# Head variances of two attention passes: VectorE statistics in PSUM in place of ScalarE squares and VectorE sums

## The chip, the cores and the metric

The kernel runs on one NeuronCore of a Trainium2 chip. The metric is the device time of one execution in microseconds (us); lower is better. Five engines take part, each with its own queue of instructions that run in order: TensorE (PE in the profile, its weight loads PEld), VectorE (DVE), ScalarE (ACT), GpSimd (POOL) and SyncE (SP), which issues the DMAs. They wait for one another by semaphores alone.

## What is computed

A gated block over 16 sequences of 64 tokens with 256 features. A first cross attention and a feed-forward layer come ahead of what matters here. Then one attention layer runs twice over the 1024 tokens, as a pass over the block's own keys and values and as a cross pass over those of a context; an expert layer ends the kernel. The part that the change touches, cut from the reference:

```python
def _ln(x, w, b):
    mu = jnp.mean(x, axis=-1, keepdims=True)
    var = jnp.mean(jnp.square(x - mu), axis=-1, keepdims=True)
    return (x - mu) * jax.lax.rsqrt(var + EPS) * w + b
...
q = _fp8_linear_pertensor(ln_out, wq, wq_scale, q_in_scale).reshape(b, s, g, hpg, d)
q = _ln(q, qln_w, qln_b)
k = _fp8_linear_pertensor(ln_out, wk, wk_scale, k_in_scale).reshape(b, s, g, d)
k = _ln(k, kln_w, kln_b)
v = _fp8_linear_pertensor(ln_out, wv, wv_scale, v_in_scale).reshape(b, s, g, d)
core = _gqa(q, k, v).reshape(b, s, nh * d)
qx = _fp8_linear_pertensor(ln_out, wqx, wqx_scale, qx_in_scale).reshape(b, s, g, hpg, d)
qx = _ln(qx, qxln_w, qxln_b)
kvx = jnp.einsum('bsi,oi->bso', cond, w_kv_x)
```

There are 16 query heads and 8 key heads of d = 128 columns. Each head of each token is normalised by its own variance (`_ln`) before the scores.

## The kernel before

**Tiles.** A tile is 128 tokens (two sequences); each pass has 8 tiles, numbered 0 to 7 (own) and 8 to 15 (cross). A tile's projections come in chunks of 512 columns, four heads, each in one PSUM bank. In the own pass these are, by the index `i`: key 0, query 0, query 1, key 1, query 2, query 3 (the six that are normalised) and two chunks of values. In the cross pass only the four query chunks 1, 2, 4 and 5 are projected; keys and values are loaded from DRAM, where the start of the kernel has put them, and the keys' variances are made beforehand from a second load (`key_squares`, `key_sums`, `key_rstd`). The weights are centred per head when they are split, so that a head's mean is zero and its variance is the mean of its squares.

**The variance of a chunk, three engines long.** ACT squares the bank into SBUF (`square`, L1979), scaled so that the 128 squares of a head and one further column that holds epsilon add up to the variance plus epsilon. DVE adds the 129 columns of each of the four heads (`sums`, L1727). POOL raises the four results to the power -1/2 (`rstd`, L1615) into `g_rs`. Buffers for four such chunks are used in turn (`NORMS`).

**The scale, then the turn.** The chunk is multiplied by its heads' factors into `g_qn`: ACT does chunks 0 and 3 as four activations of 128 columns with a factor each (L2005), DVE does the query chunks 1, 2, 4 and 5 as one multiplication of 512 columns (L1740). PE transposes `g_qn` (`turn`, L2247), and ACT keeps the result, multiplied by the norm's weight and with its bias added (`keep_qk`, L2013, parameters `lnp`). `g_qn` has two buffers, so a scale waits for the turn of two chunks before. A PSUM bank is projected into again only after the scale of the chunk that it held.

**The rest of a tile.** Scores (L2258), the row maxima and their subtraction on DVE (L1746, L1750), the exponential on ACT (L2023), its sums on DVE (L1756), the division on POOL (`normalise`, L1625), a transpose of the probabilities (L2267), which ACT keeps (`keep_pT`, L2032), the product with the values (`attend`, L2284), then on DVE the rounding to fp8 in steps (`unload`, `clip`, `power`, `lift`, L1766 to L1782), finished on POOL (`g_cat`, L1636), and the output projection (L2303).

**The order is written out by hand** for each engine: `ahead(0)` starts tile 0, `both_own(n)` interleaves the attention of tile n with the projections of tile n + 1 = m, and `both_cross(n)` does so from n = 7 on. `ahead` also holds, among the work of tile 0, the context products (L2225), which ACT copies out (`keep_context`, L1986), and the rounding of token blocks on DVE (`round_tokens`, L1787 to L1795). In `both_own(1)`, `(3)` and `(5)` POOL centres a chunk of the cross pass's weights (`ctx.centre`, L185) between two `rstd` and `normalise`. Where several engines scale, `after_scale` makes a reader wait for the count of the engine that scaled the chunk: `kn_done` counts ACT's scales, `qn_done` DVE's. SP loads a tile's keys for the cross pass behind `kn_done`.

## Time and profile before

| | us |
|---|---|
| median of 3 runs | 634.34 (633.56 to 635.05) |
| span of the profiled execution, first to last instruction | 632.0 |
| PE busy in it | 576.7 |
| DVE busy | 494.6 |
| ACT busy | 369.1 |
| POOL busy | 365.9 |

The span is that of one profiled execution; what lies before the first and behind the last instruction of a run is not in it. A busy share is a mean over stages with different limits. Matmuls are pipelined, so PE that is busy is not PE at its peak, and the ends of matmuls are modelled. In the views below every line begins with a time in us from the start of the span, or with a line of the kernel; "out<-in" names what is written and read with sizes (partitions x elements), and "idle before <-releaser" is the time that the engine stood still ahead of the group and whose work ended it.

### The profile page before, as it was taken

The numbers are of one execution on the slowest core, as the hardware profiler recorded it, in microseconds if no ns is written. First come the engines' busy times: TensorE is split into PE (matmuls) and PEld (weight loads), VectorE is DVE, ScalarE is ACT, GpSimd is POOL, SyncE is SP. The second block draws the span as 40 slices with busy tenths as digits, with TensorE's granted clock in tenths as the row PEclk, the third lists the DMA queues.
The fourth block names the chain that finished last, engine by engine and source line by source line (L and its number), as shares of the span: only waits on it lengthen the run. The fifth ranks groups of instructions, "written<-read, shape, count | busy, mean of one in ns | idle before, by whom it ended". The sixth has DMA issues, their size and how long they took to land.

```text
span 632.0 us, 10614 instructions
## 1 busy us (share of the span) xinstructions
PE 576.7 (91%) x3735; PEld 468.2 (74%) x3738; DVE 494.6 (78%) x924; ACT 369.1 (58%) x669; POOL 365.9 (58%) x299
## 2 busy tenths in 40 slices
PE   3999679959869999999988999999999999999996
PEld 1664225635548888988977889888889888888886
DVE  4697999775999998999998889999997956333333
ACT  1559657757766776776766676667665235434221
POOL 4101495014578787868659967676777634855431
PEclk9999999988989999999998999999999999999999
DMA  7892113015512131031192141222210100310001
GB/s 219 272 348 77 60 50 117 34 67 152 180 33 106 35 111 58 1 134 35 48 357 96 37 124 57 86 84 85 59 43 18 35 0 3 117 37 30 1 2 67
DMA packets 44564, 54.87 MB, mean 87 GB/s; under 512 B 8416, under 2 KB 30816, under 8 KB 44512
## 3 DMA queue, kind: packets, MB, share of 16 engines
q1 hardware_dynamic: 44512, 54.20, 26.5%
q8 instruction: 30, 0.49, 0.3%
q14 instruction: 22, 0.18, 0.1%
HBM read 41.60 MB, written 12.58 MB: 86 GB/s over the span
## 4 chain that ended last, share of the span: by engine, by line
PE 64%; DVE 6%; POOL 3%; issue 3%; ACT 2%; DVEq 0%; POOLq 0%; ACTq 0%
PE g_proj L2217 13%; PE g_proj L2303 8%; PE g_scores L2258 7%; PE g_turn L2247 6%; PE g_op L2284 5%; PE g_op L474 3%; PE g_op L475 2%; PE g_op L476 2%; PE g_proj L459 2%; PE g_proj L461 2%; PE g_proj L460 2%; PE g_turn L2267 2%; PE g_op L2225 1%; POOL g_rs L1615 1%; PE g_turn L459 1%
## 5 line engine op out<-in xcount | busy, mean ns | idle before, releaser
L1615 POOL TENSOR_TENSOR g_rs<-g_ve,neg_half 128x4 f32<-128x4 f32 x80 | 83.7, 1052 | 36.4 <-DVE g_ve L1727 36.0
L1636 POOL TENSOR_TENSOR g_cat<-g_yb,g_kb 128x1024 fp32r<-128x1024 bf16 x32 | 70.9, 2224 | 41.3 <-DVE g_yb L1782 41.3
L2217 PE MATMUL g_proj<-w_hi,g_xqc 128*128 128x512 f32 x192 | 84.4, 439 | 6.7 <-ACT g_qn L2005 4.1
L2217 PE MATMUL g_proj<-w_lo,g_xqc 128*128 128x512 f32 x192 | 76.2, 397 | 0.0
L503 POOL TENSOR_TENSOR m_h_lo<-m_h,m_h_hi 128x512 fp32r<-128x512 f32 x32 | 41.4, 1297 | 57.1 <-ACT m_h_hi L490 57.1
L1727 DVE TENSOR_REDUCE g_ve<-g_sq 128x4 f32<-128x516 f32 x80 | 54.8, 685 | 16.9 <-ACT g_sq L1979 14.9
L2258 PEld LDWEIGHTS g_scores<-g_qkT 128*128 128x128 f32 x512 | 60.9, 192 | 2.7 <-issue 1.4
L2258 PE MATMUL g_scores<-g_qkT 128*128 128x64 f32 x512 | 61.0, 272 | 0.0
L2247 PE MATMUL g_turn<-ident,g_qn 128*128 128x128 f32 x384 | 58.2, 278 | 1.8 <-DVE g_qn L1740 1.5
L1979 ACT ACTIVATE g_sq<-g_proj 128x512 f32<-128x512 f32 x80 | 47.8, 597 | 16.7 <-PE g_proj L2217 15.2
L2247 PEld LDWEIGHTS g_turn<-ident,g_qn 128*128 128x128 f32 x384 | 44.8, 143 | 11.7 <-DVE g_qn L1740 3.6
L490 ACT ACTIVATE m_h_hi<-m_h 128x512 fp32r<-128x512 f32 x32 | 20.2, 632 | 48.6 <-DVE m_h L497 48.6
L2217 PEld LDWEIGHTS g_proj<-w_hi,g_xqc 128*128 128x128 f32 x192 | 36.8, 191 | 15.6 <-ACT g_qn L2005 5.0
L2013 ACT ACTIVATE g_qkT<-g_turn,c_lnp 128x512 f32<-128x512 f32 x48 | 36.6, 778 | 16.6 <-PE g_turn L2247 16.6
L1323 PE MATMUL f_bank<-f_w_ctx,f_ctxT 128*128 128x512 f32 x96 | 44.0, 594 | 0.9 <-ACT f_kept L1079 0.9
L1740 DVE TENSOR_TENSOR g_qn<-g_proj,g_rs 128x512 f32<-128x512 f32 x64 | 43.7, 682 | 1.3 <-POOL g_rs L1615 1.3
L2284 PE MATMUL g_op<-g_pT,g_v 64*128 64x128 f32 x512 | 37.2, 285 | 5.5 <-ACT g_pT L2032 5.5
L513 DVE SCALAR_TENSOR_TENSOR x_res<-g_op,m_we,x_res 128x256 f32<-128x256 f32 x64 | 27.8, 479 | 17.8 <-PE g_op L476 17.8
L2284 PEld LDWEIGHTS g_op<-g_pT,g_v 64*128 64x128 f32 x512 | 31.1, 187 | 14.4 <-ACT g_pT L2032 9.9
L555 POOL TENSOR_TENSOR ln_rstd<-ln_ve,neg_half 128x4 f32<-128x4 f32 x6 | 6.5, 1085 | 60.3 <-DVE ln_ve L542 60.3
L2217 PEld LDWEIGHTS g_proj<-w_lo,g_xqc 128*128 128x128 f32 x192 | 36.9, 192 | 5.6 <-issue 1.0
L2013 ACT ACTIVATE g_qkT<-g_turn,x_lnp 128x512 f32<-128x512 f32 x48 | 36.2, 771 | 5.6 <-PE g_turn L2247 5.6
(242 smaller groups left out, 1662.2 us busy)
## 6 DMA issues: line engine op xcount, KB each, us to landing
kvx_rows<-f_kept SPq DMA_DIRECT2D x24, 256.0 KB, 2.4
g_ksq<-kvx_rows SPq DMA_DIRECT2D x8, 512.0 KB, 4.5
g_kraw<-kvx_rows SPq DMA_DIRECT2D x16, 256.0 KB, 3.2
g_v<-kvx_rows SPq DMA_DIRECT2D x8, 512.0 KB, 4.2
m_raw<-in_L_W SPq DMA_DIRECT2D x16, 256.0 KB, 3.0
c_raw<-in_L_wqT SPq DMA_DIRECT2D x4, 512.0 KB, 6.2
f_w_ctx<-in_L_wkvxT SPq DMA_DIRECT2D x4, 512.0 KB, 8.0
c_praw<-in_L_wprojT SPq DMA_DIRECT2D x4, 512.0 KB, 5.6
```

Source lines behind the costliest of these rows:

```text
L1323: last = T.matmul(context_bank(e)[:], ctxT[:, c_, tile * P:(tile + 1) * P], w_ctx[:, chunk, c_, :], start=c_ == 0, stop=c_ == KT - 1)
L1615: G.tensor_tensor(rs[:, at % NORMS, :], ve[:, at % NORMS, :], k["half"][:, 0:4], ALU.pow).then_inc(q["rs_done"], 1)
L1636: G.tensor_tensor(cat[:, h].rearrange("p h (b s) -> p b h s", b=2), yb[:, h, :].rearrange("p (b h s) -> p b h s", b=2, s=SEQ), kb[:, h, :] ...
L1727: V.tensor_reduce(ve[:, at % NORMS, :], sq[:, at % 2], AX.X, ALU.add).then_inc(q["ve_done"], 1)
L1740: V.tensor_tensor(qn[:, i % 2, :].rearrange("p (h d) -> p h d", d=D), bank(n, i)[:].rearrange("p (h d) -> p h d", d=D), bcast(rs[:, at % N ...
L1979: A.activation(sq[:, at % 2, :, 0:D], bank(n, i)[:].rearrange("p (h d) -> p h d", d=D), ACT.Square, scale=D ** -0.5).then_inc(q["sq_done"], 1)
L2013: A.activation(qkT[:, n % 2, at:at + 4, :], turns[TURN_BANK[i]][:].rearrange("p (h m) -> p h m", h=4), ACT.Identity, bias=lnp[:, w + 1:w + ...
L2217: last = T.matmul(bank(n, i)[:], xqc[:, n % 2, view * KT + c_, :], w[:, c_, :], start=c_ == 0 and part == 0, stop=c_ == KT - 1 and part == 1)
L2247: last = T.transpose(out, qn[:, i % 2, h * D:(h + 1) * D], k["ident"][:])
L2258: last = T.matmul(sp_[:, (g * 2 + b) * SEQ:(g * 2 + b + 1) * SEQ], qkT[:, n % 2, 2 * kv + b, :], qkT[:, n % 2, HEADS + kv, rows], start=Tr ...
L2284: last = T.matmul(op[:, b, g * P:(g + 1) * P], v[rows, n % 2, kv * D:(kv + 1) * D], pT[rows, h, g, :], start=True, stop=True)
L2303: last = T.matmul(proj[OUT_BANK][:, 0:E], cat[:, h, hd % (2 * GH), :], w[hd // 4][:, hd % 4, :], start=hd == 0 and part == 0, stop=hd == H ...
```

## The change

- ACT's squares of both passes are gone, and with them their SBUF buffer; a filler of the same size keeps the addresses behind it.
- In their place DVE takes two statistics a chunk (`bn_stats`) straight from the PSUM bank, each over two heads of 128 columns, read in turn, column by column, so that its even elements are one head and its odd elements the other. One statistic gives, for its even and for its odd elements, a count, a mean and the sum of squared deviations.
- POOL takes the four sums of squared deviations (elements 2 and 5 of each six), adds 128 epsilon into `vp`, waits for that, and takes the power. This yields the factor without the square root of 128, by which the norm's weight (`lnp`) is multiplied once instead: two further small DVE operations on the own pass's weights, one on the cross pass's.
- ACT scales chunks 0, 2, 3 and 5 of each tile, DVE chunks 1 and 4. Counts and waits follow (`act_scales`, `after_scale`).

The diff, cut to its core:

```diff
+        for w in (0,) if self.cross else (0, 2):
+            V.tensor_scalar(self.lnp[:, w:w + 1], self.lnp[:, w:w + 1], D ** 0.5, None, ALU.mult).then_inc(self.scales, 1)
...
-        sq = sb("sq", [P, 2, 4, D + 1])
-        ve, rs, qn = sb("ve", [P, NORMS, 4]), sb("rs", [P, NORMS, 4]), sb("qn", [P, 2, CH])
+        sb("unused", [P, 984])
+        ve, vp = sb("ve", [P, NORMS, 2, 6]), sb("vp", [P, NORMS, 4])
+        rs, qn = sb("rs", [P, NORMS, 4]), sb("qn", [P, 2, CH])
...
+        def act_scales(n):
+            return (0, 2, 3, 5)
...
# rstd(n, i), POOL
-                    G.tensor_tensor(rs[:, at % NORMS, :], ve[:, at % NORMS, :], k["half"][:, 0:4], ALU.pow).then_inc(q["rs_done"], 1)
+                    G.tensor_scalar(vp[:, at % NORMS, :].rearrange("p (a b) -> p a b", b=2), ve[:, at % NORMS, :, 2::3], D * LN_EPS, None,
+                                    ALU.add).then_inc(q["vp_done"], 1)
+                    pool.wait_ge(q["vp_done"], at + 1)
+                    G.tensor_tensor(rs[:, at % NORMS, :], vp[:, at % NORMS, :], k["half"][:, 0:4], ALU.pow).then_inc(q["rs_done"], 1)
...
# sums(n, i), DVE
-                    dve.wait_ge(q["sq_done"], at + 1)
+                    dve.wait_ge(q["qkv_done"], projected(n, i))
                     if at >= NORMS:
                         dve.wait_ge(q["rs_done"], at - NORMS + 1)
-                    V.tensor_reduce(ve[:, at % NORMS, :], sq[:, at % 2], AX.X, ALU.add).then_inc(q["ve_done"], 1)
+                    for two in range(2):
+                        heads = bank(n, i)[:, two * 2 * D:(two + 1) * 2 * D].rearrange("p (h d) -> p d h", d=D)
+                        last = V.bn_stats(ve[:, at % NORMS, two, :], heads)
+                    last.then_inc(q["ve_done"], 1)
...
# ahead(n), DVE: scale(n, 2) and scale(n, 5) go; ACT:
-                    square(n, 0)
-                    square(n, 1)
                     scale(n, 0)
                     keep_context(1)
                     own_out.high(act, 2)
-                    square(n, 2)
                     keep_qk(n, 0)
                     keep_context(2)
                     over_scale(2)
-                    square(n, 3)
                     keep_qk(n, 1)
-                    square(n, 4)
                     keep_context(3)
+                    scale(n, 2)
                     scale(n, 3)
                     keep_qk(n, 2)
-                    square(n, 5)
...
                     for u in range(4, 8):
                         over_scale(u)
+                    scale(n, 5)
                     keep_qk(n, 4)
...
# both_own(n), DVE: scale(m, 2) and scale(m, 5) go; ACT, squares left out:
                     keep_qk(m, 0)
                     keep_pT(n, 0)
                     keep_qk(m, 1)
+                    scale(m, 2)
                     scale(m, 3)
                     keep_pT(n, 1)
                     keep_qk(m, 2)
                     keep_v(m, 0)
                     keep_qk(m, 3)
+                    scale(m, 5)
                     keep_qk(m, 4)
...
# both_cross(n), ACT: the same, scale(m, 2) ahead of scale(m, 3), scale(m, 5) last
```

## Rows read from the trace of the kernel before

**Rows 1.** The page: PE's busy time, share of the span, instructions.

```profile
PE 576.7 (91%) x3735; PEld 468.2 (74%) x3738; DVE 494.6 (78%) x924; ACT 369.1 (58%) x669; POOL 365.9 (58%) x299
```

**Rows 2.** Table by stretch: length, busy PE, PEld, DVE, ACT, POOL, clock, DMA.

```profile
247.50:268.20 20.70, 20.40 (x159) 17.83 (x158) 19.13 (x31) 14.53 (x28) 16.38 (x14) 1.00 0.09 26
268.20:289.60 21.40, 21.40 (x165) 18.80 (x164) 19.98 (x34) 14.96 (x29) 16.20 (x14) 1.00 0.29 99
...
410.77:429.48 18.71, 18.01 (x152) 16.32 (x151) 17.08 (x33) 12.16 (x26) 13.27 (x13) 1.00 0.24 71
```

**Rows 3.** Chain of waits, 264 to 311 us: start, length, work.

```profile
264.36 3.85 PE g_proj L2303 x32
...
281.49 1.86 PE g_proj L2217 x8
...
285.76 1.97 POOL g_rs L1615 x2
287.74 1.87 POOL x_raw L185
...
290.66 0.66 PE g_turn L2267 x4
```

**Rows 4.** Instructions in order of time, 154 to 186 us: start, length, engine, work.

```profile
154.18 0.60 PE L2247 MATMUL g_turn<-ident,g_qn 128*128 128x128 f32 x4
...
155.54 0.60 PE L2247 MATMUL g_turn<-ident,g_qn 128*128 128x128 f32 x4
...
157.60 0.59 ACT L1986 ACTIVATE g_late_kept<-g_op 128x512 f32<-128x512 f32 x1
...
174.37 0.69 DVE L1727 TENSOR_REDUCE g_ve<-g_sq 128x4 f32<-128x516 f32 x1 [1.22 <-ACT g_sq L1979]
...
175.80 0.69 DVE L1727 TENSOR_REDUCE g_ve<-g_sq 128x4 f32<-128x516 f32 x1 [0.74 <-ACT g_sq L1979]
...
185.25 0.50 PE L2217 MATMUL g_proj<-w_hi,g_xqc 128*128 128x512 f32 x1 [1.36 <-DVE g_qn L1740]
```

**Rows 5.** Groups by form, from 130 us: count, busy us, mean ns, idle before.

```profile
L1727 DVE TENSOR_REDUCE g_ve<-g_sq 128x4 f32<-128x516 f32 x80 | 54.8, 685 | 16.9 <-ACT g_sq L1979 14.9 <-issue 0.2
L1740 DVE TENSOR_TENSOR g_qn<-g_proj,g_rs 128x512 f32<-128x512 f32 x64 | 43.7, 682 | 1.3 <-POOL g_rs L1615 1.3
...
L328 DVE BATCH_NORM_STATS2 m_stats<-x_res 128x6 f32<-128x256 f32 x8 | 3.3, 413 | 0.0
...
L1979 ACT ACTIVATE g_sq<-g_proj 128x512 f32<-128x512 f32 x80 | 47.8, 597 | 16.7 <-PE g_proj L2217 15.2
...
L2005 ACT ACTIVATE g_qn<-g_proj,g_rs 128x128 f32<-128x128 f32 x64 | 18.3, 369 | 19.7 <-POOL g_rs L1615 19.7
```

**Rows 6.** Instructions in order of time on DVE, near 116 us.

```profile
116.34 1.41 DVE L536 BATCH_NORM_STATS2 ln_sums<-x_res 128x6 f32<-128x256 f32 x4
```

**Rows 7.** Groups by form on POOL, its smallest operations.

```profile
L310 POOL TENSOR_SCALAR_AFFINE_SELECT m_earlier<-m_earlier 128x49 f32<-128x49 f32 x1 | 0.3, 295 | 0.1
...
L1643 POOL MEMSET g_ksq<- 128x8 f32 x1 | 0.1, 108 | 0.0
```

**Rows 8.** Instructions in order of time on POOL, end of an own tile.

```profile
281.17 4.62 POOL L1636 TENSOR_TENSOR g_cat<-g_yb,g_kb 128x1024 fp32r<-128x1024 bf16 x2 [2.65 <-DVE g_yb L1782]
```

**Rows 9.** An own tile: POOL's second normalise, then PE in the chain of waits.

```profile
273.42 1.05 POOL L1625 TENSOR_TENSOR g_ex<-g_ex,g_rc 128x512 f32<-128x512 f32 x1
...
274.90 0.44 PE g_turn L2267 x4
```

**Rows 10.** Instructions in order of time, chunks 1 and 2 of an own tile.

```profile
271.48 0.77 ACT L2013 ACTIVATE g_qkT<-g_turn,c_lnp 128x512 f32<-128x512 f32 x1
...
273.33 0.66 PE L2247 MATMUL g_turn<-ident,g_qn 128*128 128x128 f32 x4
```

**Rows 11.** Instructions in order of time on ACT, a cross tile.

```profile
412.90 1.27 ACT L2005 ACTIVATE g_qn<-g_kraw,g_krs 128x128 f32<-128x128 f32 x4
...
415.27 0.60 ACT L2032 ACTIVATE g_pT<-g_turn 128x512 f32<-128x512 f32 x1 [0.28 <-PE g_turn L2267]
```

More of the change, by code:

```diff
@@ L192, in high @@
             act.wait_ge(self.loaded[n], 16)
-        act.wait_ge(self.scales, 4 if self.cross else 6)
+        act.wait_ge(self.scales, 5 if self.cross else 8)
         for c_ in range(KT):
@@ L1496, in after_scale @@
                 return
-            if i in (0, 3):
-                eng.wait_ge(q["kn_done"], n * 2 + i // 3 + 1)
-            else:
-                eng.wait_ge(q["qn_done"], n * NP + (1, 2, 4, 5).index(i) + 1)
+            act = i in act_scales(n)
+            done = sum((i_ in act_scales(n_)) == act for n_ in range(n + 1) for i_ in range(NN if n_ < n else i + 1))
+            eng.wait_ge(q["kn_done"] if act else q["qn_done"], done)
         def measured(n, i):
@@ L1639, in ahead @@
                 def ahead(n):
-                    G.memset(sq[:, :, :, D:D + 1], LN_EPS).then_inc(q["eps_made"], 1)
                     copy_tile(0)
@@ L1822, in ahead @@
                     early_tokens()
-                    dve.wait_ge(q["eps_made"], 1)
                     sums(n, 0)
@@ L1829, in ahead @@
                     sums(n, 2)
-                    scale(n, 2)
                     sums(n, 3)
@@ L1838, in ahead @@
                     late_tokens(1)
-                    scale(n, 5)
                 def both_own(n):
@@ L1860, in both_own @@
                     sums(m, 3)
-                    scale(m, 2)
                     sums(m, 4)
@@ L1869, in both_own @@
                     clip(n, 1)
-                    scale(m, 5)
                     power(n, 1)
@@ L1888, in both_cross @@
                     less_max(n, 1)
-                    scale(m, 2)
                     if n == TILES - 1:
@@ L1905, in both_cross @@
                     unload(n, 1)
-                    scale(m, 5)
                     clip(n, 1)
@@ L1972, in _ @@
                 A = nc.scalar
-                def square(n, i):
-                    at = measured(n, i)
-                    act.wait_ge(q["qkv_done"], projected(n, i))
-                    if at >= 2:
-                        act.wait_ge(q["ve_done"], at - 1)
-                    A.activation(sq[:, at % 2, :, 0:D], bank(n, i)[:].rearrange("p (h d) -> p h d", d=D), ACT.Square,
-                                 scale=D ** -0.5).then_inc(q["sq_done"], 1)
                 def keep_context(e):
@@ L1992, in scale @@
                 def scale(n, i):
-                    half = CHUNKS[i][1]
-                    if cross(n):
+                    kind, half = CHUNKS[i]
+                    if cross(n) and kind == "k":
                         act.wait_ge(q["krs_done"], n - TILES + 1)
@@ L2118, in both_cross @@
                         key_squares(n)
-                    square(m, 1)
                     exponent(n, 0)
-                    square(m, 2)
                     if n in (TILES - 1, TILES):
@@ L2130, in both_cross @@
                         moe.high(act, MATRIX[n])
-                    square(m, 4)
                     keep_qk(m, 1)
+                    scale(m, 2)
                     scale(m, 3)
-                    square(m, 5)
                     keep_pT(n, 1)
@@ L2138, in both_cross @@
                         moe.keep(act, TOKENS[n], proj[OUT_BANK])
+                    scale(m, 5)
                 ahead(0)
```

21 lines of the change are left out of this document (7 added, 14 removed).

## The prediction, made before the change was run

> **What bounds the kernel now.** I read the page first: TensorE (PE) is busy 91% of a span of 632.0 us [rows 1]. A share over the whole span hides which stage has which limit, so next comes the table by stretch, one attention tile to a line [rows 2]. An even own-pass tile lasts 20.70 us with PE busy 20.40 and VectorE (DVE) 19.13; an odd one 21.40 with DVE 19.98; a later cross-pass tile 18.71 with PE 18.01 and DVE 17.08. So PE fills the tiles and DVE is close behind. The chain of waits shows which of the two ends last [rows 3]: from 264.36 to 283.35 it is PE alone, 19 pieces end to end (the first and the last are shown). Only in odd tiles does it leave PE, for POOL: two `g_rs` powers, the centring of a weight chunk, the softmax multiply, and PE's transpose at 290.66. An odd tile is 0.70 us longer than an even one, which is all that this stall costs. Before 185 us it is otherwise: there PE restarts behind a DVE scale, at 185.25 after 1.36 us of waiting [rows 4].
>
> So the trace says: work taken from DVE or ScalarE (ACT) inside a tile buys nothing unless it shortens the POOL stall of three odd tiles or the start before 185 us; work added costs nothing until DVE passes the length of a tile.
>
> **Part 1, what goes and comes.** All counts and means are from the grouped rows [rows 5]. ACT loses 80 squares of 0.597 us (47.8) and gains 32 query chunks of four 128-column scales; 64 such scales, 16 chunks, took 18.3 us, so 1.14 a chunk and 36.6 in all. DVE loses 80 sums of 0.685 (54.8) and 32 scales of 0.682 (21.8), and gains 160 statistics of 256 columns. POOL gains 80 adds on four numbers a partition.
>
> **The price of a statistic.** One on 256 columns of SBUF took 0.413 [rows 5], and four in a row took 1.41 [rows 6], so each further one 0.333 and a pair 0.75. No row has one that reads PSUM, nor any DVE read that steps from column to column, which the interleaving of two heads does (512 bytes away and back). That it is PSUM is no matter: the scale reading PSUM took 0.682 and the sum reading SBUF 0.685, both over 512 columns. The stepping is open. Below: 0.333 each. Above: as if all 512 columns of the bank were passed for each, 0.685 each, a pair 1.37. I take 0.75 a pair, because the nearest row is the same operation over the same count, and keep 1.37 for a rival.
>
> Here a rule of the Trainium skill speaks against the change: "Advanced Engine Details and Errata", section PSUM Cachelines, says that PSUM has lines of 8 bytes, two fp32 values, that every two consecutive elements should be contiguous, and that a pattern that is not slows matmuls much. It names no figure for DVE, and no row shows it either way; if it holds for DVE's reads it is rival C, priced there from rows. By the taken price the sum is the forecast below, by the rule it is C's.
>
> **DVE's load.** An own tile: six pairs for six sums, 6 x (0.75 - 0.685) = +0.4, less two scales, -1.36: about -1.0. A cross tile: 4 x 0.065 - 1.36 = -1.1. DVE falls from 19.13 to about 18.2 of 20.70. PE covers all of that, so it is worth nothing by itself.
>
> **POOL's add and its wait.** The add must land before the power, so each `g_rs` becomes two dependent operations, and everything behind them on POOL (normalise, centre, copies, `g_cat`) is later. POOL's smallest rows are a memset of 8 columns, 0.108, and a select of 49, 0.295 [rows 7]; with a hand-over of under 0.1 I take 0.27 for the add, from 0.15 to 0.5. In odd tiles two of them stand in the stalled chain: +0.54. Against it, this chain begins with `g_cat`, at 281.17, released by DVE's lift [rows 8]; a scale of 0.68 (chunk 5) stood in front of that lift and moves to ACT, while the pair before costs 0.07 more: `g_cat` starts 0.6 earlier. Together 0.0 for each of three odd tiles (-0.3 to +0.5). In even tiles the chain never touches POOL. Its second normalise is the tighter one: it ends at 273.42 + 1.05 = 274.47, and PE comes to its transpose at 274.90 [rows 9], 0.4 later; two adds stand ahead of it, of which the second waits for DVE anyway, so up to 0.5 is set against 0.4 and I cost it at 0.
>
> **The scale of chunk 2 on ACT.** PE transposes it at 273.33; ACT's keep of the chunk before begins at 271.48 and takes 0.77 [rows 10]. Behind that the scale ends at 271.48 + 0.77 + 1.14 = 273.39 and PE follows 0.05 later: a slip of 0.05 to 0.1 in each of seven own tiles, +0.4. ACT has the room since the three squares around it are gone. In a cross tile ACT's key scales now begin behind it: 412.90 + 1.14 + 1.27, less up to two overlaps of 0.1, is 415.1 to 415.3, and the keep of the probabilities, for which PE waits before its second attend, begins at 415.27 [rows 11]. That is +0.05 a tile with bounds 0 and 0.15; eight tiles, +0.4. Chunk 5's scale waits for chunk 3's transpose and stands ahead of the next key scale and three keeps, later by up to its own 1.14; PE has a projection and a block of scores to do before it wants the first of them, so I cost it at 0, and at up to 0.5 a tile should that cover be short. The load of the next keys hangs on the key scales' count, now four a tile in place of two, and moves with them, outside the chain.
>
> **The start, 141 to 185 us.** Two things against each other [rows 4]. Against: in tile 0 ACT comes to chunk 2 only behind chunk 1's keep and a copy of the context. Chunk 1's transpose ends at 154.78, then 0.77 + 0.59 + 1.14, less overlap: PE transposes chunk 2 at about 157.2 and not at 155.54, 1.65 later, and chunk 4's projection behind it. The square that followed (0.60 and its hand-over) is gone, so DVE's chain starts 1.0 later. For: on the way to 185.25 one scale of 0.68 leaves DVE, and the waits for squares, 1.22 and 0.74, can go in part: a square's own 0.60 of each. Two pairs before them and one extra small operation (0.15) add 0.3. I take -0.9 at the second sum of tile 1, of which POOL's weight splits, on which DVE's roundings wait there, give back most, and then +0.4 because chunk 2 of tile 1 is again behind ACT. Sum -0.2, bounds -1.5 and +1.5.
>
> **Between the passes** the same `g_cat` sets the chain, 0.6 earlier, less one pair and one add: -0.2. The two extra operations on weights in the own pass (0.15 each, at 31 us) are under other work: 0, or +0.3 without it.
>
> **Sum.** -0.2 + 0.0 + 0.4 + 0.4 - 0.2 = +0.4 on a span of 632.0, which gives 632.4. The median of the runs, 634.34, is 2.34 above the span; I hold that constant: 634.7. About 0.2% (1.3 us) is what a measurement of this kernel can tell from no change, so this is "the same".
>
> **The rivals.**
> A, the forecast: the pair costs under 1.1, PE stays the bound, 634.7 (633 to 637).
> B, faster: the add is at its cheap end, so that three odd tiles lose 0.3 each, and at the start the square's waits go in full while the slip of chunk 2 lies beside the context products: -0.9 - 1.5 and no ACT slips, 631.9. For it: DVE idles 1.96 us for squares there. Against: ACT's order in tile 0.
> C, slower, the stepped read. DVE decides from the point where a pair eats its room: an even tile has 20.70 - 19.13 + 1.36 = 2.93 us, over six chunks 0.49, so from a pair of 0.685 + 0.49 = 1.17 on. At 1.37 an own tile holds 19.13 - 1.36 + 6 x 0.685 = 21.9 us of DVE work, an odd one 22.7: +1.2 and +1.3, over seven tiles +8.7. A cross tile: 17.08 - 1.36 + 4 x 0.685 = 18.5 of 18.71, still covered. At the start four pairs stand in DVE's chain, +2.7, less the scale, already counted. 634.7 + 8.7 + 2.7 = 646. The rule on PSUM's lines that the Trainium skill gives would have it so. For it in the rows: none steps through PSUM, so none excludes it. Against: the DVE rows over 512 fp32 columns agree within 0.01 us, whichever memory they read [rows 5].
> D, slower, POOL: an add of 0.5 puts +0.5 on three odd tiles and, as chunks 2 and 3 both stand ahead of the second normalise, eats 0.5 us against 0.4 of room in the other tiles, and ACT's slips are at their upper ends (0.1 x 7, 0.15 x 8): 638.
>
> **Chances.** A 0.44, B 0.20, C 0.26, D 0.10. A's own spread reaches below 633.1 for 0.06, stays within for 0.26, and goes above 635.6 for 0.12. Faster: 0.20 + 0.06 = 0.26. Same: 0.26 + 0.02 from D = 0.28. Slower: 0.12 + 0.26 + 0.08 = 0.46. Faster and slower together hold most, so beside A's own 633 to 637 stands the range that takes in B and most of C: 631.5 to 647.
>
> **What would show it.** The line of the new statistics: a mean near 0.41 is A, 0.65 or more C; then DVE's busy time in an even own tile near 18.2 or near 22. The POOL add: 0.1 to 0.3. The chain of waits between two even tiles: PE alone (A), or DVE statistics in it (C). Tile 0: chunk 2's transpose near 157.2. Odd tiles: the transpose of probabilities still waiting for POOL by about 0.3. I am wrong if own tiles change by over 0.3 us with a mean under 0.5, or if the start moves by over 1.5.

## The result, and the profile after

The changed kernel takes 643.41 us, the median of its runs (642.8 to 644.18), where the kernel before took 634.15 beside it. The ratio is 1.0141, with a 95% interval of 1.0115 to 1.0167: slower by 9.3 us. The time lies inside the range of 631.5 to 647 but 8.7 us above the forecast of 634.7, and the reason for which the range reached so far, a slow stepped read, is not what happened: that the range held is luck. The span went from 632.0 to 641.3.

First the page of the changed kernel, as in [rows 1]: PE's work is the same, but its share of the span fell.

```profile
PE 578.3 (90%) x3738; PEld 469.7 (73%) x3738; DVE 486.5 (76%) x975; ACT 361.0 (56%) x717; POOL 389.7 (61%) x378
```

Its groups by form, which answer to [rows 5] (mean ns of one behind the busy time, then the idle time ahead):

```profile
L1622 POOL TENSOR_TENSOR g_rs<-g_vp,neg_half 128x4 f32<-128x4 f32 x80 | 88.0, 1100 | 6.7
...
L1735 DVE BATCH_NORM_STATS2 g_ve<-g_proj 128x6 f32<-128x256 f32 x160 | 59.6, 415 | 14.2 <-PE g_proj L2201 14.0
...
L1749 DVE TENSOR_TENSOR g_qn<-g_proj,g_rs 128x512 f32<-128x512 f32 x32 | 22.0, 688 | 6.7 <-POOL g_rs L1622 6.2 <-issue 0.3
L1619 POOL TENSOR_SCALAR g_vp<-g_ve 128x4 f32<-128x4 f32 x80 | 21.5, 268 | 29.5 <-DVE g_ve L1735 29.1
```

The statistic reads PSUM in steps of 512 bytes and takes 415 ns, against 413 from SBUF in one run of columns. The addition on POOL takes 268 ns. Both prices are the ones taken. What is new stands at the ends of the lines: DVE's scales now wait 6.2 us for POOL, where [rows 5] has 1.3.

The table by stretch, with the columns of [rows 2] (the clock, 1.00 here, stands ahead of the last two): two own tiles, even and odd, and a cross tile. The own stretches begin at other points of a tile than those of [rows 2], so their lengths are not compared one with one.

```profile
207.65:229.00 21.35, 21.35 (x164) 18.79 (x164) 18.39 (x36) 14.35 (x32) 17.36 (x19) 1.00 0.09 26
229.00:250.34 21.34, 20.42 (x159) 17.90 (x158) 19.38 (x39) 12.97 (x29) 18.67 (x19) 1.00 0.30 99
419.13:438.57 19.44, 17.95 (x156) 16.32 (x154) 16.46 (x34) 12.12 (x30) 14.49 (x18) 1.00 0.23 68
```

DVE has less to do, and the tiles are longer all the same. To see in which stage the time went, one needs a mark that every tile has: the start of DVE's first maximum of the tile's scores. Four of them from the timeline of the changed kernel (tiles 1, 7, 8 and 15):

```profile
197.26 0.68 DVE L1755 TENSOR_REDUCE g_mx<-g_scores 128x8 f32<-128x512 f32 x1
...
326.39 0.69 DVE L1755 TENSOR_REDUCE g_mx<-g_scores 128x8 f32<-128x512 f32 x1 [0.69 <-PE g_scores L2242]
...
351.56 0.69 DVE L1755 TENSOR_REDUCE g_mx<-g_scores 128x8 f32<-128x512 f32 x1
...
486.26 0.68 DVE L1755 TENSOR_REDUCE g_mx<-g_scores 128x8 f32<-128x512 f32 x1
```

The same four marks in every kernel of this study give the stages, in us of the profiled execution. "Ratio" is to the kernel before on the same chip, with its 95% interval.

| kernel | to tile 1 | own, 1 to 7 | 7 to 8 | cross, 8 to 15 | rest | time, median | ratio |
|---|---|---|---|---|---|---|---|
| before | 197.46 | 126.59 | 24.04 | 129.42 | 154.49 | 634.15 | 1 |
| after | 197.26 | 129.13 | 25.17 | 134.70 | 155.04 | 643.41 | 1.0141 [1.0115, 1.0167] |
| e1: cross chunk 2 scaled by DVE | 198.02 | 129.16 | 25.17 | 129.76 | 154.59 | 637.92 | 1.0062 [1.0050, 1.0074] |
| e2: cross chunk 2 earlier on ACT | 198.12 | 129.16 | 24.98 | 129.76 | 154.58 | 638.28 | 1.0059 [1.0047, 1.0071] |
| e3: no addition | 195.87 | 125.39 | 23.61 | 134.58 | 155.55 | 637.07 | 1.0060 [1.0039, 1.0080] |
| e4: all query scales on DVE | 196.49 | 131.59 | 25.71 | 129.91 | 154.30 | 639.82 | 1.0088 [1.0075, 1.0101] |
| e8: e4 without addition | 198.01 | 126.62 | 24.11 | 128.99 | 154.77 | 634.12 | 0.9989 [0.9977, 1.0000] |
| e10: e2 without addition | 198.72 | 125.44 | 24.65 | 128.99 | 155.10 | 633.39 | 0.9965 [0.9947, 0.9983] |
| e11: moves alone, with squares | 198.00 | 129.68 | 24.24 | 129.54 | 155.24 | 638.44 | 1.0059 [1.0040, 1.0079] |
| e5: e2, scalar addition on DVE | 196.33 | 134.38 | 24.16 | 132.41 | 154.62 | 646.63 | 1.0178 [1.0154, 1.0203] |
| e6: as e5, own pass only | 199.16 | 134.38 | 25.40 | 129.71 | 154.55 | 643.97 | 1.0141 [1.0117, 1.0164] |
| e7: e6, tile 0 scaled by DVE | 198.78 | 134.06 | 24.87 | 129.77 | 154.62 | 643.99 | 1.0137 [1.0112, 1.0161] |
| e9: e2, sum of two on DVE, own pass | 197.91 | 125.46 | 25.46 | 129.83 | 154.54 | 634.88 | 1.0009 [0.9992, 1.0026] |
| e12: as e9, both passes | 198.12 | 125.48 | 24.86 | 130.37 | 154.67 | 634.45 | 0.9998 [0.9984, 1.0011] |

How far to trust a column: after, e1 and e2 are the same up to tile 7, and their own pass agrees within 0.03 us, but their first column spreads over 0.9; e3 and e10 are the same up to tile 7 too, and their own pass agrees within 0.05, their first column only within 2.9. So the two passes are read to a tenth, the first column not below 3 us. TensorE's granted clock goes with this: in every kernel of the table it is 1.00 throughout both passes, and lower ahead of tile 1 and between the passes, where PE stands still for a while. There two kernels can differ by the clock as well as by their work. In the stretch between the passes, before and after:

```profile
324.05:348.09 24.04, 19.54 (x149) 17.35 (x147) 21.55 (x34) 15.19 (x29) 18.70 (x13) 0.93 0.52 169
326.39:351.56 25.17, 20.16 (x144) 17.74 (x142) 21.00 (x35) 14.59 (x33) 19.33 (x17) 0.86 0.50 159
```

A mean of 0.93 or 0.86 of full speed means that PE ran at 1.2 GHz for a part of the stretch and at 2.4 for the rest; the fall came within or just behind a wait of PE for POOL's `g_ex`, of 3.2 us before and 3.5 after.

The loss from before to after: -0.2 to tile 1, +2.5 in the own pass, +1.1 between the passes, +5.3 in the cross pass, +0.6 behind: 9.3. The last of these was not followed.

### The profile page after: what moved, and what is told of

Same layout as the page of the kernel before. It is cut to its first block, busy times and chain, and to the rows that moved or that the text cites. A ratio compares the mean times of both kernels' runs of the same rounds, so it can differ in the third digit from the quotient of the medians.

```text
span 641.3 us, 10716 instructions
## 1 busy us (share of the span) xinstructions
PE 578.3 (90%) x3738; PEld 469.7 (73%) x3738; DVE 486.5 (76%) x975; ACT 361.0 (56%) x717; POOL 389.7 (61%) x378
## 4 chain that ended last, share of the span: by engine, by line
PE 49%; POOL 12%; issue 7%; DVE 5%; ACT 3%; DVEq 0%; POOLq 0%; ACTq 0%
PE g_proj L2201 7%; PE g_proj L2287 6%; POOL g_rs L1622 5%; PE g_scores L2242 4%; PE g_turn L2231 4%; PE g_op L476 2%; POOL g_cat L1643 2%; PE g_op L477 2%; PE g_op L478 2%; PE g_proj L461 2%; PE g_op L2268 2%; PE g_proj L463 2%; PE g_proj L462 2%; PE g_op L2209 2%; ACT g_qn L1999 2%
## 5 line engine op out<-in xcount | busy, mean ns | idle before, releaser
L1622 POOL TENSOR_TENSOR g_rs<-g_vp,neg_half 128x4 f32<-128x4 f32 x80 | 88.0, 1100 | 6.7
L1999 ACT ACTIVATE g_qn<-g_proj,g_rs 128x128 f32<-128x128 f32 x192 | 54.6, 370 | 35.1 <-POOL g_rs L1622 30.9
L1735 DVE BATCH_NORM_STATS2 g_ve<-g_proj 128x6 f32<-128x256 f32 x160 | 59.6, 415 | 14.2 <-PE g_proj L2201 14.0
L2231 PE MATMUL g_turn<-ident,g_qn 128*128 128x128 f32 x384 | 56.9, 277 | 3.6 <-ACT g_qn L1999 3.3
L2026 ACT ACTIVATE g_pT<-g_turn 128x512 f32<-128x512 f32 x32 | 19.1, 597 | 45.2 <-PE g_turn L2251 45.2
```

The lines of the kernel that those rows point to most:

```text
L1622: G.tensor_tensor(rs[:, at % NORMS, :], vp[:, at % NORMS, :], k["half"][:, 0:4], ALU.pow).then_inc(q["rs_done"], 1)
L1735: last = V.bn_stats(ve[:, at % NORMS, two, :], heads)
L1999: last = A.activation(qn[:, i % 2, h * D:(h + 1) * D], source[:, h * D:(h + 1) * D], ACT.Copy, scale=by[:, h:h + 1])
L2231: last = T.transpose(out, qn[:, i % 2, h * D:(h + 1) * D], k["ident"][:])
```

## The cross pass: a bank held on ACT

PE's waits in the cross pass (335 to 500 us; total, times, longest) begin, in the changed kernel, with a line that the kernel before does not have there:

```profile
PE g_proj L2201 <- ACT g_qn L1999: 6.5, 8, 0.8
PE g_op L2268 <- ACT g_pT L2026: 5.5, 8, 0.7
```

The second line is old. The kernel before has, in the same window:

```profile
PE g_op L2284 <- ACT g_pT L2032: 5.5, 8, 0.7
```

The chain of waits of the changed kernel shows one of the eight, in order of time:

```profile
417.97 0.45 PE g_turn L2231 x4
418.42 0.02 issue
418.45 0.02 ACT g_qkT L2007
...
419.13 1.14 ACT g_qn L1999 x4
420.26 0.04 issue
420.31 1.20 PE g_proj L2201 x4
```

PE turns chunk 1, ACT keeps it, only then does ACT scale chunk 2, and PE's next projection starts when that scale ends. It is chunk 5's: in the cross pass chunks 2 and 5 share a PSUM bank (`CTX_BANK = {1: 1, 2: 0, 4: 1, 5: 0}`), and `project_context(n, 5)` waits for the scale of chunk 2 (`after_scale(pe, n, i - 3)`). Theory T1 is that this is the cross pass's loss. Two runs tell whether it is who scales, where in the queue, or neither.

**e1**, in the cross pass alone:

```diff
-            return (0, 2, 3, 5)
+            return (0, 3, 5) if cross(n) else (0, 2, 3, 5)
...
                     less_max(n, 1)
+                    scale(m, 2)
...
                     keep_qk(m, 1)
-                    scale(m, 2)
                     scale(m, 3)
```

> One edit to the changed kernel: in the cross pass only, chunk 2 is scaled by DVE again, after less_max(n, 1), and ACT scales chunks 0, 3 and 5 there. Everything else of the change stays. Theory T1 (the gate is the bank that chunks 2 and 5 share: chunk 2's scale stands on ACT behind keep_qk(m, 1), and PE's projection of chunk 5 waits 0.8 us for it, 7 to 8 times): the cross pass gives back 8 x 0.8 = 6.4 us, time about 637 (635.5 to 638.5), the wait of g_proj on ACT's g_qn disappears from the cross window, and the time of an own tile stays. Rival R1 (the statistics and POOL's addition slow the cross pass, not who scales): time stays at 643 to 644. Rival R2 (DVE gets late when it has the scale back beside the statistics): 640 or more, with a new wait on DVE's g_qn.

Measured: 637.92; the cross pass falls from 134.70 to 129.76, the own pass stays at 129.16.

**e2**, the scale stays on ACT:

```diff
+                    scale(m, 2)
                     keep_qk(m, 1)
-                    scale(m, 2)
                     scale(m, 3)
```

> One edit to the changed kernel: in both_cross ACT's scale(m, 2) stands ahead of keep_qk(m, 1) and not behind it; ACT still does both. T1 with its cause in the order of ACT's queue (the factor is ready well before, ACT stands idle in between, and keep_qk(m, 1) waits for chunk 1's turns): PE's wait for the bank goes, about 637 (636 to 639). Rival R3 (ACT's own 1.14 us for four instructions, against 0.68 on DVE, is what makes chunk 5 late, wherever it stands): at most 0.4 x 8 = 3 us come back, 640 to 642. Rival R1: 643 to 644.

Measured: 638.28, the cross pass again 129.76. PE's waits in the cross pass of this kernel no longer have the line:

```profile
PE g_op L2268 <- ACT g_pT L2026: 5.5, 8, 0.7
PE g_turn L2251 <- POOL g_ex L1632: 3.8, 2, 3.4
```

ACT's 1.14 us do no harm; the place behind `keep_qk(m, 1)` does. T1 holds for the mechanism, and R1 to R3 fall. The size was 4.9 us and not the 6.4 that eight waits of 0.8 suggested: of the eight one lies ahead of the mark of tile 8, the other seven come to 5.6, and a wait of 0.4 for POOL takes a part of their place. 0.3 us over the kernel before stay in the cross pass.

## The own pass: POOL's addition

Theory T2 blames the addition. **e3** leaves it out (and with it epsilon):

```diff
-                    G.tensor_scalar(vp[:, at % NORMS, :].rearrange("p (a b) -> p a b", b=2), ve[:, at % NORMS, :, 2::3], D * LN_EPS, None,
-                                    ALU.add).then_inc(q["vp_done"], 1)
-                    pool.wait_ge(q["vp_done"], at + 1)
-                    G.tensor_tensor(rs[:, at % NORMS, :], vp[:, at % NORMS, :], k["half"][:, 0:4], ALU.pow).then_inc(q["rs_done"], 1)
+                    G.tensor_tensor(rs[:, at % NORMS, :].rearrange("p (a b) -> p a b", b=2), ve[:, at % NORMS, :, 2::3],
+                                    k["half"][:, 0:4].rearrange("p (a b) -> p a b", b=2), ALU.pow).then_inc(q["rs_done"], 1)
```

> One edit to the changed kernel: POOL raises the variances to the power straight from DVE's statistics, without the addition; epsilon is left out of the computation. Theory T2 (two dependent POOL instructions for each factor delay the odd own tiles, where POOL sets the end, by 0.6 to 0.8 us each, and chunk 2's factor in the even ones): the own pass gives back 2.0 to 2.8 us and the cross pass little, time about 641 (640.3 to 641.8). Rival (the addition is hidden by slack, and the own pass is late through ACT's scale of chunk 2 alone): 643 to 643.6. If the cross pass is late through POOL too, against T1: 636 or less.

Measured: 637.07, 6.3 us below the changed kernel where 2.0 to 2.8 were expected. The own pass gives 3.7 back and stands 1.2 below the kernel before; the stretch between the passes gives 1.6; the cross pass gives 0.1. The rest of the 6.3 lies ahead of tile 1, where it is within the spread, and between the passes e3 also ran at the higher clock (0.93 against 0.86): e2 and e10, which differ by the addition alone and both have 0.86 there, take 24.98 and 24.65. So of the 1.6 only 0.3 is shown to be the addition's:

```profile
327.28:352.26 24.98, 20.73 (x147) 18.19 (x146) 20.90 (x35) 15.06 (x33) 19.31 (x17) 0.86 0.48 159
324.16:348.81 24.65, 20.79 (x147) 18.21 (x146) 20.68 (x36) 15.03 (x33) 18.18 (x13) 0.86 0.52 162
```

In the own pass T2's place is right and its price was too low: the addition had hidden a gain of the change as well as caused a loss.

How 0.27 us comes to this is read on POOL in the changed kernel. An odd tile, in order of time:

```profile
287.08 0.23 POOL L1619 TENSOR_SCALAR g_vp<-g_ve 128x4 f32<-128x4 f32 x1
287.39 1.03 POOL L1622 TENSOR_TENSOR g_rs<-g_vp,neg_half 128x4 f32<-128x4 f32 x1
288.41 0.23 POOL L1619 TENSOR_SCALAR g_vp<-g_ve 128x4 f32<-128x4 f32 x1
288.72 1.03 POOL L1622 TENSOR_TENSOR g_rs<-g_vp,neg_half 128x4 f32<-128x4 f32 x1
289.72 1.90 POOL L187 TENSOR_TENSOR x_raw<-x_raw,x_sums 128x1024 f32<-128x1024 f32 x1
```

Each addition is 0.23 us and 0.08 until POOL starts its own power: 2.64 from the first addition to the centring, where the powers alone took 1.98 (285.76 to 287.74 in [rows 3]). An even tile is worse, and DVE waits behind it (the first line is DVE's work meanwhile, the last view DVE's wait):

```profile
265.22 1.65 DVE L204 SCALAR_TENSOR_TENSOR w_lo<-x_raw,x_sc,w_hi 128x512 fp32r<-128x512 f32 x2
...
265.64 0.66 POOL L1619 TENSOR_SCALAR g_vp<-g_ve 128x4 f32<-128x4 f32 x1
266.38 1.39 POOL L1622 TENSOR_TENSOR g_rs<-g_vp,neg_half 128x4 f32<-128x4 f32 x1
267.75 0.22 POOL L1619 TENSOR_SCALAR g_vp<-g_ve 128x4 f32<-128x4 f32 x1
268.06 1.03 POOL L1622 TENSOR_TENSOR g_rs<-g_vp,neg_half 128x4 f32<-128x4 f32 x1
```

```profile
269.12 0.69 DVE L1749 TENSOR_TENSOR g_qn<-g_proj,g_rs 128x512 f32<-128x512 f32 x1 [0.93 <-POOL g_rs L1622]
```

The same pair of powers in e3 follows on itself and is through in 2.43 us; here it takes 3.45, and 0.43 of that is that the first addition itself takes 0.66 and not 0.23. Four of the 80 additions take 0.65 to 0.69, all of them beside DVE's `w_lo`; 69 take 0.25 or less. Why it is slow there was not tried. The pair in e3:

```profile
262.32 2.43 POOL L1619 TENSOR_TENSOR g_rs<-g_ve,neg_half 128x4 f32<-128x4 f32 x2
```

DVE stands still for chunk 1's factor, so its later statistics and then chunk 2's factor come later, and PE waits for ACT's scale of chunk 2. From mark to mark the even tiles 2, 4 and 6 went from 20.78, 20.77 and 21.14 us to 21.17, 21.45 and 21.92, the odd ones from 21.30 to 21.53. PE's waits of 190 to 325 us in the changed kernel, total, times, longest:

```profile
PE g_turn L2251 <- POOL g_ex L1632: 2.1, 3, 0.8
PE g_turn L2231 <- ACT g_qn L1999: 0.8, 3, 0.3
```

Together 2.9; e3 has none there, and the kernel before has this alone:

```profile
PE g_turn L2267 <- POOL g_ex L1625: 0.9, 3, 0.3
```

**e4** keeps the statistics and the addition and gives chunks 2 and 5 of every tile back to DVE, at the places of the kernel before:

```diff
-            return (0, 2, 3, 5)
+            return (0, 3)
...
                     sums(m, 3)
+                    scale(m, 2)
                     sums(m, 4)
...
                     clip(n, 1)
+                    scale(m, 5)
                     power(n, 1)
...
                     keep_qk(m, 1)
-                    scale(m, 2)
                     scale(m, 3)
```

> The changed kernel with its statistics and POOL's addition kept, but chunks 2 and 5 of every tile scaled by DVE again, at the places of the kernel before; ACT squares nothing and scales chunks 0 and 3 alone. T1 and T2 together: the cross pass gives back 6.4 us as in the run with chunk 2 alone, the own pass keeps POOL's 2 to 2.8 us, and DVE's scales beside the statistics cost 0 to 1: 636 to 638. Rival R1 (the statistics are what slows the kernel): 642 or more. If the statistics without the moves beat the kernel before (squares' waits of the start gone, ACT empty): below 633.

Measured: 639.82, above the 636 to 638 expected. The cross pass comes down as expected, to 129.91. The own pass does not: 131.59, 2.5 above the changed kernel. So in the own pass the moves to ACT help. **e8** is e4 without the addition:

> The statistics alone: ACT squares nothing, DVE's statistics, POOL's power straight from them without the addition (epsilon is left out of the computation), and all query scales on DVE as before the change. Against the run with the addition (639.8): if the addition costs as much here as in the changed kernel, 6 us less, 633.5, so that the statistics by themselves would be worth about 1 us over the kernel before. If the moves of the scales to ACT were what made the addition visible, 638 or more. Against the kernel before an own tile is expected within 0.3 us (DVE's statistics cost 0.75 where sums cost 0.69), the start 2 us shorter.

Measured: 634.12, ratio 0.9989: 5.7 us less, and level with the kernel before in the own pass (126.62 against 126.59). The 1 us that the statistics were expected to be worth is not there; a tie is all they are by themselves, and a start 2 us shorter is not seen (198.01 to tile 1, 197.46 in the kernel before), though that column can hardly tell 2 us. The moves alone, on the kernel before with its squares and sums, are **e11** (tiles 1 to 7):

```diff
+        def act_scales(n):
+            return (0, 2, 3, 5) if 0 < n < TILES else (0, 3)
...
                     square(m, 4)
+                    scale(m, 2)
                     scale(m, 3)
...
                     keep_qk(m, 3)
+                    scale(m, 5)
                     keep_qk(m, 4)
```

> The kernel before with one part of the change alone: ACT scales chunks 2 and 5 of own tiles 1 to 7; ACT's squares, DVE's sums, tile 0 and the cross pass stay as they were. With the statistics and no addition, the moves made an own pass of 125.4 us (tile 1 to 7) out of 126.6. If that is DVE's relief by 1.36 us a tile, it is there with the squares too: 633.0 (632.3 to 633.8), with PE's waits in the own pass gone. Rival (ACT, which squares 6 times 0.60 us a tile here, comes late with the scales): 635 or more.

Measured: 638.44, the rival's side. PE's waits, 190 to 325 us, in this kernel:

```profile
PE g_turn L2248 <- ACT g_qn L2004: 4.4, 7, 0.6
```

ACT, with six squares a tile still in its queue, brings a scale 0.6 us late in each of the seven tiles. The own pass in one table:

| variance by | scales of chunks 2 and 5 on DVE | on ACT |
|---|---|---|
| squares on ACT, sums on DVE | 126.59 (before) | 129.68 (e11) |
| statistics, POOL adds | 131.59 (e4) | 129.13 (after) |
| statistics, nothing added | 126.62 (e8) | 125.39 (e3) |

The two halves of the change need each other: the statistics empty ACT, which lets the moves gain 1.2 us in place of losing 3.1. POOL's addition, 3.7 to 5.0 us over these six tiles, takes that and more.

## Where else the addition can be done

If 0.35 us on POOL is the trouble, DVE could add. **e5** does so in all tiles, **e6** in own tiles only, both with e2's order:

```diff
# rstd(n, i), POOL: the addition and its wait go. sums(n, i), DVE:
...
-                    last.then_inc(q["ve_done"], 1)
+                    last.then_inc(q["vp_done"], 1)
+                    dve.wait_ge(q["vp_done"], at + 1)
+                    V.tensor_scalar(vp[:, at % NORMS, :].rearrange("p (a b) -> p a b", b=2), ve[:, at % NORMS, :, 2::3], D * LN_EPS, None,
+                                    ALU.add).then_inc(q["ve_done"], 1)
```

> The changed kernel with chunk 2's scale ahead of keep_qk(m, 1) in the cross pass (as in the run before of that edit, 638.3 us) and with the addition of epsilon on DVE, right behind the second of a chunk's two statistics, for every chunk of both passes; POOL raises to the power alone. The run without the addition gained 6.3 us. Theory T2a (what costs is POOL's time and its hand-over to itself: 0.27 + 0.07 us on the engine whose order is full in the own pass): most of it comes back, 633 (632 to 635), and DVE's wait for POOL's g_rs in the own pass (6.2 us in 10 waits) is gone or halved. Theory T2b (what costs is the latency of a second dependent instruction, on whichever engine): DVE's addition takes an estimated 0.2 us and a hand-over, and 2 us at most come back, 636 to 638. Rival (DVE becomes the bound: 24 + 32 more instructions beside its 18.4 us an own tile): 638 or more.

> As the last, but DVE adds epsilon in the own pass and POOL still in the cross pass. The run without any addition left the cross pass as it was (134.6 against 134.7 us), so POOL's addition should cost nothing there: T2a gives 633 (632 to 635), the same as with DVE adding everywhere or up to 1 us less, if DVE's 4 more instructions a cross tile show. If the addition on POOL does cost in the cross pass once chunk 2's scale is out of the way, this one is the slower of the two, by 0.5 us or more.

Measured: 646.63 and 643.97. Every theory expected a gain or, for the third, a loss from 48 or 80 short instructions; the own pass grew to 134.38, by 5.2. DVE's timeline in e6, in an odd tile:

```profile
245.13 0.75 DVE L1736 BATCH_NORM_STATS2 g_ve<-g_proj 128x6 f32<-128x256 f32 x2
245.92 2.10 DVE L1742 TENSOR_SCALAR g_vp<-g_ve 128x4 f32<-128x4 f32 x1
247.93 0.75 DVE L1736 BATCH_NORM_STATS2 g_ve<-g_proj 128x6 f32<-128x256 f32 x2
248.71 0.17 DVE L1742 TENSOR_SCALAR g_vp<-g_ve 128x4 f32<-128x4 f32 x1
```

The same instruction takes 0.17 and, ahead of it, 2.10 us, ending at 248.02. POOL at that moment:

```profile
243.36 4.62 POOL L1644 TENSOR_TENSOR g_cat<-g_yb,g_kb 128x1024 fp32r<-128x1024 bf16 x2 [2.05 <-DVE g_yb L1798]
```

These are two subtractions. The second by itself is this, and it ends at 247.98, within 0.04 us of the addition:

```profile
245.87 2.11 POOL L1644 TENSOR_TENSOR g_cat<-g_yb,g_kb 128x1024 fp32r<-128x1024 bf16 x1
```

The short one, at 248.71, runs beside a `g_rs` power of POOL (248.16 to 249.17). **e7** is e6 with tile 0's two scales on DVE:

```diff
-            return (0, 2, 3, 5)
+            return (0, 3) if n == 0 else (0, 2, 3, 5)
```

> As the last (epsilon on DVE in the own pass, chunk 2's scale ahead of keep_qk(m, 1) in the cross pass), and tile 0's chunks 2 and 5 are scaled by DVE at their places in the kernel before: ACT scales them from tile 1 on. In the run with all scales back on DVE tile 0's first key maximum came 28.5 us after the first product of the own pass, against 30.9 in the changed kernel and 30.4 in the kernel before. Theory: this gives back 1.9 to 2.4 us, 631 (630 to 632.5), which would be below the kernel before. Rival (the start was better there through something else, or the time is lost again in tile 1): no difference to the last run.

Measured: 643.99, no difference. Tile 0's first maximum came 30.35 us after the first product of the pass in place of 31.21, about as much as two kernels with the same start differ (30.35 in e1, 31.17 in e2). The 28.5 of e4 was followed by a longer tile 0 (26.85 us against 24.99 in the changed kernel): the rival.

**e9** adds by another kind of instruction, a sum over the variance and a constant beside it, in own tiles; POOL adds in the cross pass:

```diff
...
+                    V.tensor_reduce(vp[:, at % NORMS, :].rearrange("p (a b) -> p a b", b=2),
+                                    ve[:, :, at % NORMS, :, 2::3].rearrange("p e a b -> p a b e"), AX.X, ALU.add).then_inc(q["ve_done"], 1)
```

> DVE adds epsilon in the own pass again, but by another kind of instruction: a sum over two elements (the variance and a constant laid out beside it) in place of the addition of a scalar; chunk 2's scale stands ahead of keep_qk(m, 1) in the cross pass, where POOL still adds. In the two runs before, the scalar addition took 0.17 us except at chunk 0 of each own tile, where it took 2.1 us and ended with the first of POOL's two g_cat subtractions. The Trainium skill (SBUF - State Buffer, the part on the shared port pair) says that an instruction of DVE with one SBUF input in a 2-port mode waits for a GpSimd instruction that holds the pair, that the addition of a scalar can be in such a mode, and that a sum never is. Theory T3 (the 2.1 us are the wait for POOL's subtraction, and belong to the kind of instruction): the sum takes 0.1 to 0.25 us everywhere, the own pass from tile 1 to tile 7 takes 125.4 to 127.5 us where the scalar addition gave 134.4 and POOL's addition 129.2, and the time is 633 (632 to 635.5). Rival (any instruction that follows the statistics there is late, or the third instruction of a chunk loads DVE too much): 636 to 644, with the 2 us still in the rows.

Measured: 634.88. DVE's sum, beside a `g_cat` of POOL that lasts from 239.00 to 243.62:

```profile
241.56 0.17 DVE L1743 TENSOR_REDUCE g_vp<-g_ve 128x4 f32<-128x8 f32 x1
```

```profile
239.00 4.62 POOL L1644 TENSOR_TENSOR g_cat<-g_yb,g_kb 128x1024 fp32r<-128x1024 bf16 x2 [2.05 <-DVE g_yb L1799]
```

0.17 us where the addition of a scalar took 2.10, in the same place and with the same neighbour. T3 holds: it is the kind of instruction. (The expectation says that the 2.1 us ended with the first of the two subtractions; it was the second.) The own pass is 125.46, as good as with no addition (125.39). So T2a, which e5 and e6 seemed to refute, holds in the own pass: a second dependent instruction on DVE costs nothing there that can be told, so it was POOL's time, and not the dependence, that cost. All 48 sums took 0.17 us, 12 of them within a `g_cat`.

**e12** uses the sum in both passes:

> The run before with DVE's sum of two (0.17 us) in the cross pass as well; POOL adds nothing. That run stood at 634.9 against 634.8 for the kernel before, with 25.46 us between tile 7 and tile 8 and 129.83 us from tile 8 to tile 15. The two kernels without any addition took 24.1 and 24.65 us between the tiles and 128.99 us in the cross pass, so POOL's addition seems to cost there too once chunk 2's scale is out of the way, by 0.8 to 1.3 and 0.8 us. Theory: this comes back, time 633.0 (632.3 to 633.8), just below the kernel before. Rival (DVE, with 32 more instructions a pass, is late by as much in the cross pass): 634.5 to 635.5, and a cross pass of 129.8 us or more. The scalar addition on DVE in both passes gave a cross pass of 132.4 us: if the sum gives that too, it is the third instruction, and not its kind, that costs there.

Measured: 634.45, ratio 0.9998. The cross pass is 130.37, 0.5 above e9: the rival. There POOL's addition is the cheaper one, and e5's scalar addition costs 2.0 more than the sum (132.41): in e5 the second addition of a cross tile takes 0.69 us and the third mostly 0.8 to 1.0, ending with a `g_ex` of POOL.

**e10** has e2's order and no addition (epsilon left out), to see whether the two losses are separate:

> Both repairs at once: chunk 2's scale ahead of keep_qk(m, 1) in the cross pass, and no addition at all (epsilon is left out of the computation). One gave 5.1 us back, the other 6.3. If the two losses are separate (one lies in the cross pass, the other in the own pass and between the passes), they add up: 643.4 - 5.1 - 6.3 = 632.0 (631.2 to 632.8), just below the kernel before. Rival (the two repairs overlap in the cross pass): 633.5 or more.

Measured: 633.39, 1.4 above what was expected and below the kernel before by 0.35%. The passes add up as expected (own 125.44, and cross 128.99, better than either repair). So the two losses are separate there, and the addition costs 0.8 in the cross pass too once the bank is free (e2 has 129.76). The missing 1.4 us and more lie ahead of tile 1, where this profiled execution is 2.9 us behind e3's, and up to there the two programs are the same. What differs is the granted clock, as tile 0 shows, e3 first:

```profile
171.24:195.87 24.63, 19.12 (x131) 15.58 (x130) 23.68 (x42) 16.95 (x35) 16.72 (x13) 0.93 0.39 128
173.21:198.72 25.51, 20.65 (x131) 17.14 (x130) 23.60 (x41) 16.72 (x35) 16.51 (x13) 0.80 0.38 125
```

The runs of e10 go the same way: the four with a mean clock of 0.982 or more over the run took 630.4 to 632.2 us, the eight with 0.980 or less 631.9 to 634.6. So the miss does not speak against the two repairs; what sets the clock ahead of tile 1 was not tried.

No kernel that computes everything is faster than the kernel before by what can be told here. e9 and e12 win 1.1 us in the own pass and lose it between the passes (25.46 and 24.86 against 24.04) and in the cross pass. Between the passes the kernels in which POOL adds in tile 8 take 24.9 to 25.7, the others 23.6 to 24.9. The clock parts them too: it is 0.93 there in before, e3, e5, e7 and e8, and 0.86 to 0.87 in the others, e9 and e12 among them. What each of the two is worth was not tried further.

## Why the prediction was wrong where it was, point by point

**The price of a statistic** was right: 415 ns, a pair 0.75. Rival C, which made the range reach to 647, is refuted, and with it the reading of the rule on PSUM's lines for DVE: the Trainium skill ("Advanced Engine Details and Errata", PSUM Cachelines) speaks of matmuls, and the trace shows no cost of the stepped read on DVE. With C the reason for the wide range is gone, and 643.41 lies in it by luck.

**DVE's load** fell as worked out in the even stretch shown (18.39 for "about 18.2"), by less from mark to mark: its busy time over the six own tiles went from 117.4 to 113.7, 0.6 a tile where about 1.0 was worked out. That it was "worth nothing by itself" is half right. With the statistics and nothing added, the moves gave 1.2 us in the own pass: PE's wait of 0.3 for POOL in each of the three odd tiles (0.9 in e8) is gone in e3. That is the earlier `g_cat` that the prediction set against the additions: in e3 it starts 0.55 us ahead of PE's projection (278.42 against 278.97), 0.47 earlier than before.

**POOL's addition** was the first mis-sized step. Its duration was right (0.27 forecast, 0.268 on average), the term was not: "0.0 for each of three odd tiles" and 0 in the even ones, where taking it away gave 3.7 us over the own pass. In odd tiles two additions with their hand-over cost 0.66 where 0.54 was set, and the earlier `g_cat` gave back 0.3 and not 0.6: it starts 0.39 us ahead of the projection that PE has at that point (282.49 against 282.88), where it was 0.08 before (281.17 against 281.25). DVE, which releases it, now waits for POOL itself, 6.2 us in ten waits. PE's wait for the probabilities grew from 0.3 to as much as 0.8. (The odd tile's stall was also misread: in [rows 2] the stretch called odd has PE busy for all of its 21.40 us, and the one called even holds the wait. From mark to mark an odd tile is 0.5 us longer than an even one, and PE's wait is 0.3 of it, so the 0.70 is not the stall's price.) In the even tiles the step was "the second waits for DVE anyway". It does not there: POOL is behind, at 3.45 us for two factors, and DVE is what waits, 0.93. The even tiles hold 1.85 of the own pass's 2.54 us, the odd ones, to which the term was given, 0.69. The working treated the addition as length on one chain; it sits in a loop, POOL to DVE to POOL, that runs through every tile.

**Chunk 2 on ACT in the own pass** was costed at +0.4 and is no loss: the moves gain there.

**Chunk 2 on ACT in the cross pass** was the step that failed outright: +0.4, where order alone was worth 4.9. The slip of the probabilities that the 0.4 was for did not come: PE's wait for them is 5.5 us in both kernels. The prediction followed the scale to its turn and to the keep of the probabilities. It did not ask who waits for the bank that the scale reads. Chunk 5's projection does, and while DVE did the scale it had long been done: in the kernel before the projections of chunk 5 wait for nothing in the cross pass. The rule was among the sentences ahead of the prediction, that a bank is projected into again only after the scale of the chunk that it held, and was not applied to this move.

**The start** came out at -0.2 to tile 1 for -0.2, but with a spread of up to 2.9 between equal programs that shows nothing of its terms. Chunk 2 of tile 0 is turned behind ACT, as worked out ("about 157.2"):

```profile
157.11 0.66 PE L2231 MATMUL g_turn<-ident,g_qn 128*128 128x128 f32 x4 [1.46 <-ACT g_qn L1999]
```

**Between the passes** -0.2 was forecast and +1.1 came. The addition is shown to be worth 0.3 there (e2 against e10); the granted clock, 0.86 in place of 0.93, came with it, and the rest stays open between the two. The working had no term for the clock.

**The rivals.** B, an addition that costs little and no slip on ACT, needed 631.9. e10, which has no addition and no slip on ACT, stands at 633.39, but B's gain at the start is not shown. D had POOL's part of the mechanism at 638, and e1 and e2, in which POOL's part is all that is left, stand at 637.92 and 638.28; but that is luck in the number: D needed an add of 0.5 us, which measured 0.27, named the cross pass's slip at 0.15 a tile, and saw neither the bank nor the loop. The sign that the prediction named for its own failure, own tiles changed by over 0.3 us with a mean under 0.5, is what the trace shows: even tiles by 0.4 to 0.8.

## What to carry to other kernels

When an operation moves to another engine's queue, list all who wait for it, those for its input's buffer too, and the instruction that it will stand behind; the cheap repair is then its place in that queue, not its engine. A short instruction between two engines that hand work to and fro is priced by taking it away: here 0.27 us of POOL, six times a tile, cost 3.7 to 5.0 us in six tiles. Before a half of a change is put down as a loss, run the halves apart: the moves lost 3.1 us with the squares, and gained 1.2 without them. And before a stretch is put down to a change, its granted clock is read beside its length.

## What the hardware showed that was not expected

An addition of a scalar on four numbers a partition took 0.17 us on DVE, and 2.10 when POOL was in `g_cat`; it ended within 0.04 us of POOL's subtraction. A sum over two numbers in the same place took 0.17 beside a running `g_cat`. The Trainium skill ("SBUF — State Buffer", on the port pair that DVE and GpSimd share) has it so: an instruction with one SBUF input contends with GpSimd only in a 2-port mode, into which the addition of a scalar can enter, a sum never does on trn2, and the one that comes second is blocked until the other's end. With `g_cat` (and `g_ex` in e5) the trace agrees, though it does not show the mode itself. It does not agree for every instruction of POOL: in e6 twelve additions of a scalar lay within a `g_rs` power on four numbers and took 0.17 all the same.

A statistic of DVE that alternates between two places 512 bytes apart in PSUM took 415 ns for 256 columns, as much as one along the columns in SBUF (413).
